# A graph network layer on one core: edge pairs taken earlier step by step, four node tiles finished among them, the last sum queued ahead of two linears

## The chip, the core and the metric

One core of a Trainium2 chip. The metric is the device time in microseconds; the kernel before took 907.19 us, the median of three runs (906.26 to 907.55).

## What is computed

Each of 106,250 edges has a source, a target (the edges are sorted by target) and one of three types. For each type, the message of an edge is the ReLU of a linear map of its source's row; a node's three sums of messages and the ReLU of its own row go through a linear map chosen by the node's type, and the result is added to twice the row (once in the layer, once around it) and normalised over its 128 features.

```python
src = node_feature[edge_src]
parts = [relu(node_feature)]
for t in range(3):
    msg = relu(src @ W_e[t].T + b_e[t])
    msg = where((edge_type == t)[:, None], msg, 0)
    parts.append(segment_sum(msg, edge_dst, num_segments=6250))
agg = concatenate(parts, axis=1)
for t in range(3):
    o = agg @ W_n[t].T + b_n[t]
    updated = where((node_type == t)[:, None], o, updated)
x = layernorm(x + (updated + node_feature))
```

## The kernel before

Nodes lie in 49 tiles of 128 rows (NT = 49, the last shorter). Setup (to about 100 us) writes a table in HBM with the message of each node for each type, while GpSimd gathers 71 chunks of 128 rows of x for the "early" edges, the last 9,050 in order.

The first 97,200 edges are 90 rows of 1,080. In each row the edges of a node to itself are handled apart (the "selfs"), 128 edges with a high source number are "dense" (their x rows are picked by one-hot matmuls from an SBUF copy of the last 1,280 nodes, so they are not gathered), and 896 edges at most are left, seven chunks of 128. Two rows make one of NI = 45 iterations: 14 gathers of 128 message rows each (L719), in four groups (quarters) of 3, 4, 3 and 4. A quarter is numbered q = 4j + g.

In quarter q TensorE sums the group with one-hot matrices (sum_group, L1605), and then does what the fixed schedule puts there. GpSimd may gather group (j, g) only after the sum of group (j-1, g), since the buffer is the same. VectorE makes the one-hot of the next iteration (L1217) and adds the sums into the accumulators at a base column that is read from a table into a register (add_to, L1229; load_bases).

Beside this run the pairs. One dense pair (256 dense edges) an iteration, and one early pair in each of the first NE = 36: a turn (dense_turn L1623, early_turn L1567), masks by type on VectorE a quarter later, the matmuls that make the messages three quarters after the turn (L1636 to L1640, L1579 to L1584), a ReLU on ScalarE, and a sum and its addition after them (ADD_LATER = 5). turn_at gives the quarter of pair r; pick_at that of its picking. LEAD_FROM and LEAD_STEP make the dense pairs from 36 on come every third quarter, so that the last is turned in quarter 171.

Node tiles are finished when no sum can reach them. Tiles 0 to 40 follow the iterations at fixed quarters (tile_step), with a turn of x (finish_turn), transposes of the selfs (place_selfs), the addition of accumulators and selfs into stage (finish_acc on VectorE, L1362), a linear of nine or more matmul instructions (linear_open L1679, L1680, linear_types L1687), the choice by node type and the statistics (finish_h, L1332 to L1340), the square root on ScalarE (finish_sd, L883) and the scaling (finish_y, L1346, L1348). Tiles 41, 42, 43 and 44 are left to last_iteration, whose order is written out by hand on each engine. Only early edges reach the four extra tiles, 45 to 48; they follow the early pairs, at quarters 151, 157, 163 and 169, in the order 48 to 45, through a set of buffers of their own (z = 1), which tile 44 uses after them. On ScalarE the roots in last_iteration are taken in the order of tiles 40, 41, 42, 43, 44; its end is:

```python
                finish_sd(Z0_TILES - 1)
                finish_sd(0, 3)
                finish_sd(KE, 1)
```

SyncE's queue is one list: loads of types and dense lists for the pairs, x rows and selfs for tiles, stores. At its end (L641 to L648) it stores tile 43, reads the control flag (which says if the input fits the plan) into a register, stores tile 44 and waits for all stores.

## Time and profile before

| | us |
|---|---|
| median of three runs | 907.19 (906.26 to 907.55) |
| the profiled execution | 908.36 |
| its span, first to last instruction | 906.6 |
| TensorE matmuls busy | 717.5 |
| GpSimd busy | 674.5 |
| VectorE busy | 614.0 |
| ScalarE busy | 145.8 |

Mean granted TensorE clock 0.909 of full speed. PE is TensorE's matmuls, PEld its weight loads, DVE VectorE, ACT ScalarE, POOL GpSimd, SPq the transfers that SyncE issues. A row of a timeline gives the start and the duration in us, the engine, the line of the program, the operation, what is written from what, how many instructions are merged, and in brackets the idle time before and what ended it. Instructions overlap in a pipeline, so that starts lie closer together than durations.

### The profile page before, as it was taken

To read this page: it belongs to the slowest core of one execution; us is meant where nothing else is said; L and a number is where in the kernel's file an instruction comes from. 1 tells how busy PE (TensorE), PEld (TensorE's weight loads), DVE (VectorE), ACT (ScalarE), POOL (GpSimd) and SP (SyncE) were. 2 spreads that over 40 slices of the span, in tenths; PEclk is the share of its full clock that TensorE was granted. 3 is DMA by queue.
4 is the path that set the end of the run, shared out by engine and by line. 5 is a ranking of instruction groups with operands and counts; after the bars stand their busy time and mean duration, and the time that the engine had idled before them with its cause. 6 is when DMAs were issued, how large, how long until landed. Compare 5 with 4: busy or idle time off the path is not lost.

```text
span 906.6 us, 13972 instructions
## 1 busy us (share of the span) xinstructions
PE 717.5 (79%) x4555; PEld 601.7 (66%) x4555; DVE 614.0 (68%) x1468; ACT 145.8 (16%) x397; POOL 674.5 (74%) x718
## 2 busy tenths in 40 slices
PE   5593066896998888888888889889887798889796
PEld 3362065785877776676677777778666677778674
DVE  6999988467676557556656666665765476757756
ACT  3293100111111101101111010111111011112120
POOL 7777777777777777777777777777777777777771
PEclk9796558799999989999999999989999898989999
DMA  8495532343543344333443344335335533434321
GB/s 251 145 313 154 138 96 77 97 111 51 146 118 105 97 109 106 96 110 90 99 122 92 94 105 113 94 94 123 95 96 128 146 69 103 110 77 121 81 53 50
DMA packets 71985, 101.39 MB, mean 112 GB/s; under 512 B 18057, under 2 KB 55437, under 8 KB 71915
## 3 DMA queue, kind: packets, MB, share of 16 engines
q0 software_dynamic: 22432, 45.99, 21.9%
q1 hardware_dynamic: 46781, 50.45, 18.7%
q10 hardware_dynamic: 2702, 4.08, 1.6%
q8 instruction: 37, 0.61, 0.3%
q14 instruction: 33, 0.27, 0.1%
HBM read 87.47 MB, written 12.97 MB: 111 GB/s over the span
## 4 chain that ended last, share of the span: by engine, by line
POOL 50%; PE 20%; issue 17%; DMA 6%; DVE 5%; SPq 0%; DVEq 0%; POOLq 0%
POOL tab L719 47%; DMA tab<-message_table,idx_t 5%; PE ps L1605 4%; PE ps L1687 3%; PE ps L1623 3%; POOL xg L715 3%; PE ps L1529 2%; PE ps L1680 1%; PE ps L1640 1%; DMA dst_raw<-in_dst 1%; PE ps L1636 1%; DVE h L1335 1%; PE ps L1648 1%; DVE first_wide L999 1%; PE ps L1530 1%
## 5 line engine op out<-in xcount | busy, mean ns | idle before, releaser
L719 POOL DMA_INDIRECT tab<-message_table,idx_t x630 | 595.9, 946 | 192.0 <-issue 186.8
L1605 PE MATMUL ps<-work,tab 128*128 128x126 f32 x1260 | 183.7, 289 | 111.5 <-DMA tab<-message_table,idx_t 87.3
L1217 DVE TENSOR_TENSOR work<-key_t,ps 128x378 f32<-128x378 f32 (+1 forms) x180 | 108.8, 606 | 228.9 <-PE ps L1605 226.8
L1605 PEld LDWEIGHTS ps<-work,tab 128*128 128x128 f32 x1260 | 165.3, 201 | 128.3 <-issue 84.2
L1229 DVE TENSOR_TENSOR acc<-ps,acc 128x126 f32 (+1 forms) x306 | 96.2, 314 | 30.6 <-DVE acc L1229 7.2
L1687 PE MATMUL ps<-wn_t,stage 128*128 128x384 f32 x282 | 98.6, 486 | 0.0
L715 POOL DMA_INDIRECT xg<-in_x,esrc_t x67 | 72.6, 1084 | 20.4 <-issue 17.1
L1687 PEld LDWEIGHTS ps<-wn_t,stage 128*128 128x128 f32 x282 | 53.6, 190 | 37.4
L1623 PE MATMUL ps<-first_wide,tab 128*128 128x128 f32 x450 | 65.3, 299 | 4.6 <-DVE first_wide L1293 4.6
L1623 PEld LDWEIGHTS ps<-first_wide,tab 128*128 128x128 f32 x450 | 61.5, 215 | 5.0 <-issue 5.0
L862 ACT ACTIVATE stage<-ps 128x128 f32<-128x128 f32 x47 | 13.1, 278 | 309.9 <-PE ps L1687 291.4
L1623 PE MATMUL ps<-dense_f,tab 128*128 128x128 f32 x450 | 60.7, 285 | 0.0
L1623 PEld LDWEIGHTS ps<-dense_f,tab 128*128 128x128 f32 x450 | 57.5, 203 | 0.0
L1335 DVE SCALAR_TENSOR_TENSOR h<-ps,mask,h 128x128 f32<-128x128 f32 x147 | 51.6, 351 | 5.2
L1579 PE MATMUL ps<-we_t,emsg 128*128 128x128 f32 x216 | 36.5, 313 | 23.3 <-issue 19.1
L1579 PEld LDWEIGHTS ps<-we_t,emsg 128*128 128x128 f32 x216 | 31.7, 220 | 25.9 <-issue 21.4
L883 ACT ACTIVATE sd<-mv,eps 128x1 f32<-128x1 f32 x49 | 14.4, 294 | 208.3 <-DVE mv L1340 208.3
L1636 PE MATMUL ps<-we_t,order_f 128*128 128x128 f32 x270 | 45.5, 314 | 3.0 <-DVE acc L1229 3.0
L1529 PE MATMUL ps<-we_t,work 128*128 128x384 f32 x98 | 42.9, 521 | 3.3 <-DVEq L961 3.2
L1640 PE MATMUL ps<-we_t,order_f 128*128 128x128 f32 x270 | 44.7, 304 | 0.0
L1636 PEld LDWEIGHTS ps<-we_t,order_f 128*128 128x128 f32 x270 | 41.4, 228 | 4.2 <-issue 3.6
L849 ACT ACTIVATE dense_f<-ps 128x256 f32<-128x256 f32 x45 | 17.3, 384 | 163.8 <-PE ps L1640 163.8
(255 smaller groups left out, 1046.7 us busy)
## 6 DMA issues: line engine op xcount, KB each, us to landing
tab<-message_table,idx_t POOLq DMA_INDIRECT x630, 3.5
message_table<-tab SPq DMA_DIRECT2D x24, 384.0 KB, 4.0
dst_raw<-dense_types SPq DMA_DIRECT2D x45, 192.0 KB
wn_raw<-message_table SPq DMA_DIRECT2D x22, 384.0 KB, 3.3
src_wide<-dense_lists SPq DMA_DIRECT2D x45, 128.0 KB, 3.3
we_raw<-early_types SPq DMA_DIRECT2D x18, 192.0 KB
be_b<-early_types SPq DMA_DIRECT2D x18, 192.0 KB
xg<-in_x SPq DMA_DIRECT2D x11, 256.0 KB, 4.0
```

The lines of the kernel that those rows point to most:

```text
L715: pool.indirect_dma_start(xg[:, q, :], None, x, bass.IndirectOffsetOnAxis(ap=rows, axis=0)).then_inc(x_gathered, 16)
L719: pool.indirect_dma_start(msg[:, slot, :], None, table, bass.IndirectOffsetOnAxis(ap=rows, axis=0)).then_inc(signal, 16)
L1217: dve.tensor_tensor(hot[:, first:first + n, :].rearrange("p c (t w) -> p c t w", w=WIN), keys.broadcast_to((P, n, T, WIN)), iota_win.rearr ...
L1229: dve.tensor_tensor(cols, sums.rearrange("p (t c) -> p t c", t=T), cols, ALU.add).then_inc(added, 1)
L1335: fin_link(dve.scalar_tensor_tensor(h[z][:, :], lin_bank(z, nth)[:, t * D:(t + 1) * D], mask[:, t, at(tile)], h[z][:, :], ALU.mult, ALU.ad ...
L1529: pe.matmul(ps[:, MSG_PS + i, 0:T * D], xt[:, par, i, :], we_t[:, :], start=True, stop=False)
L1579: pe.matmul(early_made[:, 0, :], exm[:, 0, t, :], we_t[:, t * D:(t + 1) * D], start=(t == 0), stop=False)
L1605: ins = pe.matmul(sums_bank(j, g), msg[:, column, :], hot[:, column, :], start=(c == 0), stop=(c == n - 1))
L1623: ins = pe.matmul(dxt_ps[:, :, s * DENSE:(s + 1) * DENSE], dx[:, (SETS - 1 - s) * DT + k, :], donehot[s][:, k, :, :], start=(k == 0), stop ...
L1636: pe.matmul(dmsg_ps[:, 0, :], dxm[:, 0, t, :], we_t[:, t * D:(t + 1) * D], start=(t == 0), stop=False)
L1640: ins = pe.matmul(dmsg_ps[:, 1, :], dxm[:, 1, t, :], we_t[:, t * D:(t + 1) * D], start=False, stop=(t == T - 1))
L1687: ins = pe.matmul(lin, stage[z][:, i, :], wn_t[:, i, :], start=False, stop=(i == T))
```

## The change

- Pairs: pair r, dense and early alike, is turned in quarter 4r + 3 less one quarter for each five pairs, up to eight. The early pairs' other steps are now given as distances from the turn (4 for the ReLU, 5 for the sum, 6 for the addition). Base registers are loaded for the next pair after each pair, and four for the iteration.
- Extra tiles: in the order 45 to 48, each after the early pair from which on nothing reaches it (13, 21, 30 and 35), at quarters 66, 93, 127 and 146; linears at 70, 98, 130 and 150. Self rows and x are turned together (turn_extra) into other columns of bank 2, the bank of the pairs' turns; the linear uses bank 7, that of the tiles. Both get waits for it. Loads and stores are one for each tile, in slots of xg that are free then.
- A limit for each early pair (elimit, an iota) replaces one limit for all in the check of the plan.
- The end: TensorE, VectorE and SyncE have another order in the last iteration. Numbers such as KE, 1 stand for tile 44; 0, 3 for 43; Z0_TILES - 1 for 42.

```diff
...
-ORDER = [NT - 1 - n for n in range(NZ)]
+ORDER = [NA + 1 + n for n in range(KE)] + [NA]
...
-LIN_PS, FIN_XT_PS = (7, 6, 2, 5), (5, 6, 5, 3)
-LAST_LIN_PS = 4
+LIN_PS, FIN_XT_PS = (7, 7, 2, 5), (5, 2, 5, 3)
+LAST_LIN_PS, LAST_FIN_XT_PS = 4, 6
+XT_AT = (0, T * P, 0, 0)
...
-LEAD_FROM, LEAD_STEP = NE, 3
+LEAD, LEAD_EVERY = 8, 5
 def turn_at(r):
-    return NG * min(r, LEAD_FROM) + NG - 1 + LEAD_STEP * max(r - LEAD_FROM, 0)
+    return NG * r + NG - 1 - min(LEAD, r // LEAD_EVERY)
...
+E_RELU_LATER, E_SUM_LATER, E_ADD_LATER = 4, 5, 6
...
-EXTRA_FROM, EXTRA_STEP = NG * (NE + 1) + 3, 6
-EXTRAS = {EXTRA_FROM + EXTRA_STEP * k: k for k in range(KE)}
...
+LIMIT_STEP = 15
+LIMIT_FIRST = MAIN // 17 - 30
+PAIR_OF = [min(NE - 1, max(0, -(-((NA + 2 + n) * P - LIMIT_FIRST) // LIMIT_STEP) - 1)) for n in range(KE)]
+FIRST_EXTRA = 16
+def extra_at(n):
+    ready = turn_at(PAIR_OF[n]) + E_ADD_LATER
+    r = next(r for r in range(NI) if turn_at(r) + 1 >= ready and turn_at(r) >= NG * FIRST_EXTRA)
+    return turn_at(r) + 2
+EXTRA_AT = [extra_at(n) for n in range(KE)]
+LINEAR_AT = [next(q for q in range(at + 2, at + 6) if q % NG == 2) for at in EXTRA_AT]
+EXTRAS = {at: n for n, at in enumerate(EXTRA_AT)}
+EXTRA_LINEAR = {at: n for n, at in enumerate(LINEAR_AT)}
+SLOT_OF = [EXTRA_AT[n] // NG + 8 if n < KE - 1 else NT for n in range(KE)] + [NT + 1 + T]
+LOAD_LAST = NI - 5
...
+            def load_extra(n):
+                tile, slot = ORDER[n], SLOT_OF[n]
+                rows = min(P, N - tile * P)
+                sp.wait_ge(e_turned, min(NE, (slot + T + 2) // 2))
+                sp.dma_start(xg[0:rows, slot, :], x[tile * P:tile * P + rows, :]).then_inc(fin_x[1], 16)
+                sp.dma_start(self_rows(tile),
+                             table[tile * P * T:(tile * P + rows) * T, :].rearrange("(p t) d -> p t d", t=T)
+                             ).then_inc(self_extra, 16)
+            def store_extra(n):
+                tile, slot = ORDER[n], SLOT_OF[n]
+                rows = min(P, N - tile * P)
+                sp.wait_ge(fin_y[1], n + 1)
+                sp.dma_start(out[tile * P:tile * P + rows, :], xg[0:rows, slot, :]).then_inc(stored[1], 16)
...
+                for n in range(KE):
+                    if j == EXTRA_AT[n] // NG - 2:
+                        load_extra(n)
+                    if j == (LINEAR_AT[n] + 3) // NG + 1:
+                        store_extra(n)
+                if j == LOAD_LAST:
+                    load_extra(KE)
...
+            sp.wait_ge(ctl_set, 1)
+            need = sp.value_load(ctl[0:1, 0:1], min_val=0, max_val=1)
+            store_extra(KE)
             sp.wait_ge(fin_y[3], 1)
             store_fin(NA - 1)
-            sp.wait_ge(ctl_set, 1)
-            need = sp.value_load(ctl[0:1, 0:1], min_val=0, max_val=1)
-            sp.wait_ge(fin_y[1], NZ)
-            store_fin(NA, 1, 1)
             sp.wait_ge(stored[0], 16 * STORES)
-            sp.wait_ge(stored[1], 16 * 3)
...
+            pool.iota(elimit[:, :], pattern=[[0, 1]], base=LIMIT_FIRST, channel_multiplier=LIMIT_STEP,
...
-                dve.tensor_scalar(estats[:, 2:3], estats[:, 0:1], -1.0, float(EARLY_BACK), ALU.mult, ALU.add)
+                dve.wait_ge(limits_set, 1)
+                dve.tensor_tensor(estats[:, 2:3], elimit[:, :], estats[:, 0:1], ALU.subtract)
...
                 r = dense_step(q, ADD_LATER)
                 if r is not None:
-                    dense_add(r, bases_of[NG:NG + SIDES] if r <= LEAD_FROM else load_bases(r + 2, NG, NG + SIDES))
+                    dense_add(r, pair_base[0:SIDES])
+                    if r >= NE:
+                        pair_base = load_bases(r + 1, NG, NG + SIDES)
                 if dense_step(q, MASK_LATER) is not None:
                     dense_mask(dense_step(q, MASK_LATER))
-                if g == 0 and 1 <= j <= NE:
-                    early_mask(j - 1)
+                if early_step(q, MASK_LATER) is not None:
+                    early_mask(early_step(q, MASK_LATER))
...
+                i = early_step(q, E_ADD_LATER)
+                if i is not None:
+                    early_add(i, pair_base[SIDES])
+                    pair_base = load_bases(i + 1, NG, NG + SIDES + (i + 1 < NE))
...
+            def last_iteration(j, bases_of, pair_base):
                 dve.wait_ge(group_summed, NG * j + 1)
-                dense_add(j, load_bases(j + 2, NG, NG + SIDES))
+                dense_add(j, pair_base)
                 for g in range(NG):
...
                 dve.wait_ge(group_summed, NG * j + 4)
                 add_sums(j, 3, bases_of[3])
+                finish_acc(ORDER[KE], KE, 1, ALL_ADDS)
                 finish_acc(NA - 1, 0, 3, ALL_ADDS)
-                finish_acc(ORDER[KE], KE, 1, ALL_ADDS)
                 finish_h(SPLIT + 1, Z0_TILES - 1)
+                finish_h(ORDER[KE], KE, 1, slot=SLOT_OF[KE])
+                finish_y(SPLIT + 1, Z0_TILES - 1)
                 finish_h(NA - 1, 0, 3)
-                finish_y(SPLIT + 1, Z0_TILES - 1)
-                finish_h(ORDER[KE], KE, 1)
+                finish_y(ORDER[KE], KE, 1, slot=SLOT_OF[KE])
                 finish_y(NA - 1, 0, 3)
-                finish_y(ORDER[KE], KE, 1)
...
+                extras = sum(at < turn_at(i) for at in EXTRA_AT)
+                if extras:
+                    pe.wait_ge(stage_acc[1], extras)
...
+            def turn_extra(n):
+                tile, bank = ORDER[n], fin_bank(1, n)
+                rows = min(P, N - tile * P)
+                pe.wait_ge(fin_x[1], 16 * (n + 1))
+                pe.wait_ge(self_masked[1], n + 1)
+                pe.wait_ge(d_masked, sum(turn_at(r) < EXTRA_AT[n] for r in range(NI)))
+                pe.wait_ge(e_masked, sum(turn_at(i) < EXTRA_AT[n] for i in range(NE)))
+                part = self_rows(tile)
+                for t in range(T):
+                    ins = pe.transpose(ps[:, bank, t * P:t * P + rows], part[:, t, :], ident[0:rows, 0:rows])
+                ins.then_inc(self_placed[1], 1)
+                pe.transpose(ps[:, bank, XT_AT[1]:XT_AT[1] + P], xg[:, SLOT_OF[n], :], ident[:, :]
+                             ).then_inc(fin_xt[1], 1)
...
+                if behind is not None:
+                    pe.wait_ge(fin_var[1 - z], behind)
...
                 if q in EXTRAS:
-                    k = EXTRAS[q]
-                    if k == 0:
-                        pe.wait_ge(added, ADDED["early", NE - 1, 0])
-                    else:
-                        pe.wait_ge(fin_var[1], k)
-                    finish_turn(ORDER[k], k, 2, 1, first=k == 0)
+                    turn_extra(EXTRAS[q])
                 t = tile_step(q, 1)
                 if t is not None:
                     place_selfs(t, t)
-                if q - 1 in EXTRAS:
-                    place_selfs(ORDER[EXTRAS[q - 1]], EXTRAS[q - 1], 1)
                 t = tile_step(q, LINEAR_LATER)
                 if t is not None:
-                    finish_linear(t, first=t == 0)
-                if q - LINEAR_LATER in EXTRAS:
-                    finish_linear(EXTRAS[q - LINEAR_LATER], 1, first=EXTRAS[q - LINEAR_LATER] == 0)
-                if g == 0 and 2 <= j <= NE + 1:
-                    early_sum(j - 2)
+                    extras = sum(at < q for at in LINEAR_AT)
+                    finish_linear(t, first=t == 0, behind=extras if extras else None)
+                if q in EXTRA_LINEAR:
+                    n = EXTRA_LINEAR[q]
+                    done = sum(tile_step(before, LINEAR_LATER) is not None for before in range(q))
+                    finish_linear(n, 1, first=n == 0, behind=done)
+                if early_step(q, E_SUM_LATER) is not None:
+                    early_sum(early_step(q, E_SUM_LATER))
...
                 pe.wait_ge(hot_ready, NG * NI)
                 pe.wait_ge(d_hot, NI)
+                pe.wait_ge(added, ADDED["main", j, 1])
                 linear_open(KE, 1)
+                sum_group(j, 3)
                 finish_linear(Z0_TILES - 1)
-                linear_open(0, 3, first=True)
-                pe.wait_ge(added, ADDED["main", j, 1])
-                sum_group(j, 3)
-                linear_types(0, 3)
                 linear_types(KE, 1)
+                finish_linear(0, 3, first=True)
...
```

## Rows read from the trace of the kernel before

**Rows 1.** The page, part 1, TensorE: share of the span:
```profile
PE 717.5 (79%) x4555; PEld 601.7 (66%) x4555; DVE 614.0 (68%) x1468; ACT 145.8 (16%) x397; POOL 674.5 (74%) x718
```

**Rows 2.** The waits, GpSimd before its gathers: us in total, times, longest:
```profile
POOL tab L719 <- issue: 186.8, 613, 0.3
POOL tab L719 <- PE ps L1605: 5.2, 17, 0.3
```

**Rows 3.** The gathers of messages by line: ns min/median/max, first and last start:
```profile
L719 POOL DMA_INDIRECT tab<-message_table,idx_t x630: 940/945/1064, 101.4 to 888.1; - x158
```

**Rows 4.** Timeline of TensorE at the end: start us, us, engine, line:
```profile
893.97 1.05 PE L1605 MATMUL ps<-work,tab 128*128 128x126 f32 x8
...
896.08 2.20 PE L1687 MATMUL ps<-wn_t,work 128*128 128x384 f32 x6 [1.06 <-DVE work L1362]
```

**Rows 5.** Timeline of VectorE and ScalarE at the end:
```profile
895.15 0.29 DVE L1229 TENSOR_TENSOR acc<-ps,acc 128x126 f32 x1 [1.81 <-PE ps L1605]
...
901.09 1.12 DVE L1335 SCALAR_TENSOR_TENSOR h<-ps,mask,h 128x128 f32<-128x128 f32 x3
...
902.86 0.29 ACT L883 ACTIVATE sd<-mv,eps 128x1 f32<-128x1 f32 x1 [2.11 <-DVE mv L1340]
...
902.91 0.35 DVE L1348 TENSOR_SCALAR xg<-h,mv,rstd 128x128 f32<-128x128 f32 x1
...
903.39 0.35 DVE L1348 TENSOR_SCALAR xg<-h,mv,rstd 128x128 f32<-128x128 f32 x1
```

**Rows 6.** Timeline of SyncE's queue, the last two stores:
```profile
903.28 0.33 SPq L523 DMA_DIRECT2D out<-xg  x1
...
904.54 0.34 SPq L523 DMA_DIRECT2D out<-xg  x1
```

**Rows 7.** Timelines of TensorE and GpSimd, first group and the gather it frees:
```profile
115.88 1.65 PE L1605 MATMUL ps<-work,tab 128*128 128x126 f32 x6 [23.18 <-DVE work L1217]
...
118.92 0.95 POOL L719 DMA_INDIRECT tab<-message_table,idx_t  x1 [0.30 <-issue]
```

**Rows 8.** The chain that ended last, 890 to 896 us: start, duration, what:
```profile
891.39 1.94 PE ps L1687 x6
...
893.32 0.16 PE ps L1679
...
893.48 0.65 PE ps L1680 x2
...
894.13 0.90 PE ps L1605 x8
```

**Rows 9.** Timeline of GpSimd at the start:
```profile
2.02 0.13 POOL L694 IOTA limit<- 90x2 f32 x1
...
3.25 1.10 POOL L715 DMA_INDIRECT xg<-in_x,esrc_first  x1 [0.40 <-DMA esrc_first<-in_src]
```

**Rows 10.** Chain at 432 and 835 us, timelines of GpSimd and TensorE at 270:
```profile
835.50 3.47 DMA tab<-message_table,idx_t
...
839.11 1.13 PE ps L1605 x8
...
432.68 4.08 DMA tab<-message_table,idx_t
...
270.16 0.94 POOL L719 DMA_INDIRECT tab<-message_table,idx_t  x1 [0.30 <-issue]
...
272.90 0.91 PE L1605 MATMUL ps<-work,tab 128*128 128x126 f32 x6 [1.43 <-DMA tab<-message_table,idx_t]
```

**Rows 11.** Windows: busy PE, PEld, DVE, ACT, POOL; PEclk; DMA; GB/s. Linear matmuls by line:
```profile
853.00:856.00 3.00, 0.53 (x5) 0.29 (x4) 2.80 (x7) 0.00 (x0) 2.39 (x3) 1.00 0.79 244
...
858.00:859.00 1.00, 0.21 (x1) 0.24 (x2) 0.70 (x3) 0.21 (x1) 0.93 (x1) 0.76 0.25 66
...
865.00:866.00 1.00, 1.00 (x9) 1.00 (x9) 0.00 (x0) 0.00 (x0) 0.69 (x2) 0.82 0.13 33
...
L1687 PE MATMUL ps<-wn_t,stage x282: 485/486/486, 185.7 to 899.7; 128*128 128x384 f32 x141
```

More of the change, by code:

```diff
@@ L161, in dense_step, with early_step @@
     return TURNS.get(q - later)
-EXTRA_FROM, EXTRA_STEP = NG * (NE + 1) + 3, 6
-EXTRAS = {EXTRA_FROM + EXTRA_STEP * k: k for k in range(KE)}
+def early_step(q, later):
+    i = TURNS.get(q - later)
+    return i if i is not None and i < NE else None
 ACC_LATER, LINEAR_LATER, H_LATER, SD_LATER, Y_LATER = 2, 4, 5, 6, 7
-assert max(EXTRAS) + Y_LATER <= NG * (NI - 1)
+LIMIT_STEP = 15
[12 more added lines that the diff above has]
+LOAD_LAST = NI - 5
+assert all(EXTRA_AT[n + 1] > LINEAR_AT[n] + 3 for n in range(KE - 1)) and LINEAR_AT[-1] + 3 < NG * (NI - 1)
+assert all(LIMIT_FIRST + LIMIT_STEP * (PAIR_OF[n] + 1) >= (NA + 2 + n) * P for n in range(KE - 1))
+assert PAIR_OF[-1] == NE - 1 and SLOT_OF[KE] + 1 + T <= ET
 def tile_step(q, later):
@@ L454, in self_rows, with fin_bank @@
                 return rows_of[:, tile // 2 % 2, tile % 2, :].rearrange("p (t d) -> p t d", d=D)
-            first = NT + T * (NT - 1 - tile)
+            first = SLOT_OF[ORDER.index(tile)] + 1
             return xg[0:min(P, N - tile * P), first:first + T, :]
+        def fin_bank(z, nth):
+            return LAST_FIN_XT_PS if z == 1 and isinstance(nth, int) and nth == KE else FIN_XT_PS[z]
         def load_x(engine, b, par):
@@ L532, in load_selfs @@
                              ).then_inc(self_got[m % 2], 16)
-            def load_extra_selfs():
-                for tile in ORDER:
-                    rows = min(P, N - tile * P)
-                    sp.dma_start(self_rows(tile),
-                                 table[tile * P * T:(tile * P + rows) * T, :].rearrange("(p t) d -> p t d", t=T)
-                                 ).then_inc(self_extra, 16)
             def iteration(j):
-                if 2 <= j < NE:
-                    sp.wait_ge(e_made, j - 1)
-                    load_early_types(j)
+                for i in range(2, NE):
+                    if j == (turn_at(i - 2) + MAKE_LATER) // NG + 1:
+                        sp.wait_ge(e_made, i - 1)
+                        load_early_types(i)
                 for r in range(2, NI):
@@ L554, in iteration @@
                     if j == tile + 1:
+                        before = sum(SLOT_OF[n] < tile + tiles for n in range(KE))
+                        if before:
+                            sp.wait_ge(stored[1], 16 * before)
                         sp.wait_ge(e_turned, (tile + tiles + 1) // 2)
@@ L871, in mask_selfs @@
                 else:
-                    act.wait_ge(self_extra, 16 * NZ)
+                    act.wait_ge(self_extra, 16 * (ORDER.index(tile) + 1))
                 if tile == 0:
@@ L902, in quarter @@
                     mask_selfs(ORDER[EXTRAS[q + 2]])
-                if g == 3 and 1 <= j <= NE:
-                    early_relu(j - 1)
+                if early_step(q, E_RELU_LATER) is not None:
+                    early_relu(early_step(q, E_RELU_LATER))
             def last_iteration():
@@ L1357, in finish_acc @@
                 dve.wait_ge(self_placed[z], nth + 1)
+                if z == 1 and nth < KE:
+                    dve.wait_ge(stage_xt[z], nth + 1)
                 sums = acc[:, :, tile * P:(tile + 1) * P]
@@ L1619, in dense_turn @@
                     pe.wait_ge(e_masked, min(j, NE))
+                extras = sum(at < turn_at(j) for at in EXTRA_AT)
+                if extras:
+                    pe.wait_ge(stage_acc[1], extras)
                 for s in range(SETS):
@@ L1669, in finish_turn, with linear_open @@
                     pe.wait_ge(stage_acc[z], nth)
-                pe.transpose(ps[:, FIN_XT_PS[z], 0:P], xg[:, at(tile), :].rearrange("p a d -> p (a d)"), ident[:, :]
+                slot = tile if z != 1 else SLOT_OF[nth]
+                pe.transpose(ps[:, fin_bank(z, nth), XT_AT[z]:XT_AT[z] + P], xg[:, at(slot), :].rearrange("p a d -> p (a d)"), ident[:, :]
                              ).then_inc(fin_xt[z], 1)
-            def linear_open(nth, z=0, first=False):
+            def linear_open(nth, z=0, first=False, behind=None):
                 lin = lin_bank(z, nth)
@@ L1688, in linear_types, with finish_linear @@
                 ins.then_inc(fin_lin[z], 1)
-            def finish_linear(nth, z=0, first=False):
+            def finish_linear(nth, z=0, first=False, behind=None):
                 if z == 1:
                     pe.wait_ge(stage_acc[z], nth + 1)
-                linear_open(nth, z, first)
+                linear_open(nth, z, first, behind)
                 linear_types(nth, z)
```

86 lines of the change are left out of this document (38 added, 48 removed).

## The prediction

> **What bounds the kernel now.** I read the page first: TensorE has the largest busy share, 79% [rows 1], and that does not say what bounds. The waits of GpSimd do: before its 630 gathers of message rows it was idle 0.3 us each, nearly all of it its own issue; a TensorE sum ended such a gap 17 times, never a longer one than 0.3 us [rows 2]. The gathers as a group close the question: the first began at 101.4, the last at 888.1 [rows 3], so 786.7 / 629 = 1.25 us per gather, and one gather of 0.945 with its gap of 0.3 is 1.25. So from 101 to 889 us the run is one uninterrupted row of gathers with no wait of another engine in it. What the change takes off TensorE or VectorE there is worth nothing by itself; it can cost, if a gather has to wait, or help the last 18.5 us (888.1 to the span's end, 906.6).
>
> In those the reader should see three things. The sum of the last group started at 893.97, behind all the linear work queued ahead of it on TensorE [rows 4]. VectorE had been free since 893.34, waited 1.81 us for that sum, and worked without a gap from 895.15 to 903.74 [rows 5]. SyncE issued the store of tile 43 at 903.28, right behind its rows, and that of tile 44, ready at 903.74, only at 904.54 [rows 6]: between the two stands the read of the control flag into a register.
>
> **The change, part by part.**
>
> *Pairs run ahead.* Before, pair r is turned in quarter 4r+3, and from pair 36 every third quarter; after, pair r comes min(8, r//5) quarters earlier, and the last is in quarter 171 in both. No matmul is added. From quarter 147 on, 7 pairs are turned instead of 9. Cost 0, covered by the gathers as long as GpSimd isn't held. How thin that cover can be: the first group's sum ended at 115.88 + 1.65 = 117.53, and the gather that needs it began at 118.92 [rows 7], 1.4 us of room. There pairs 0 to 4 keep their places, and only one load of three registers is added ahead of the loop. In the middle some quarters now hold the making of a pair and a tile's linear, 2.75 us more [rows 8]; the end becomes thinner.
>
> *Four extra tiles early.* Their turns move from quarters 151, 157, 163, 169 to 66, 93, 127, 146, each with 2.75 us of linear [rows 8] and its transposes. The new waits: TensorE waits for the tile's loads, its masked rows and the masks of earlier pairs; the next pair's turn waits for VectorE's addition of the extra tile; the linears of both kinds wait for each other's statistics, since they share a bank. Queued behind each are the sums, and behind these the gathers. The next turn lies two quarters behind an extra tile in all four places, and the loads are queued on SyncE two iterations ahead, 28 gathers or 35 us [rows 3]. I take 0; a held gather is rival D. On SyncE the two stores of these tiles leave the last microseconds, where they were issued while the last gather was in flight; what that gives lies within the bounds of the landing below.
>
> *Base registers.* VectorE loads a pair's bases after the pair before, instead of with the iteration: as many values, beside the gathers, and not behind the last sum in either kernel. 0.
>
> *One more iota on GpSimd* ahead of its first gather, and a limit read by VectorE: 0.13 us by its like, against 0.40 us for which that gather waited for its indices [rows 9]. 0, at most 0.1.
>
> *The last sum moved ahead.* This is the term. After, the order is: open tile 44, last sum, linear 42, types of 44, all of linear 43. First S, the end of that sum, which now waits for the last gather alone. No row shows that landing, so I bound it by sums that waited for theirs. A gather begun at 835.50 took 3.47, and its sum began at 839.11, 3.61 after the gather; another took 4.08, with the same 0.14 behind it 4.22; a group of three chunks began 272.90 - 270.16 = 2.74 after its last gather [rows 10]. I take 3.61, since it is of the same group of four chunks and late in the run. With two matmuls for the last chunk (a quarter of 0.90, 0.23 [rows 8]) S = 888.1 + 3.61 + 0.23 = 891.9, with bounds of 891.1 and 892.6. TensorE is there in time: ahead of the old sum stood a linear (2.75) and an opening (0.81) that are now behind it, and 893.97 - 3.56 = 890.4. The old sum ended at 893.97 + 1.05 = 895.0 [rows 4], so it gains 3.1 us.
>
> Not all of this arrives. After S TensorE has 2.75 + 1.94 + 2.75 = 7.44 us in a row [rows 8]. Before, two types of about 2 us were left [rows 4], and VectorE was the bound. Linear 43 is done at S + 7.44 = 899.4, and 0.12 later (the sum ended at 895.03, the add began at 895.15) VectorE has it: 899.5. VectorE's own work up to there is what it was, 901.09 - 895.15 = 5.94 us [rows 5], less than the 7.44, so TensorE sets the end now. From the last tile's first multiply-add to the square root on ScalarE it is 902.86 - 901.09 = 1.77 us [rows 5]: 901.3.
>
> *A term that goes the other way.* VectorE now finishes 44 ahead of 43, but ScalarE's order is not changed: it still takes the root of 43 first, which depends on the very last statistics, and the root of 44 behind it. So the finishing of 44, which could have lain beside the root of 43, waits too. A root is 0.29 and I put the second 0.2 behind it (an estimate between 0.16 and 0.29); then 0.59 from root to the first tile's end (903.15 to 903.74) and 0.48 to the second's (903.26 to 903.74) [rows 5]: 901.3 + 0.29 + 0.2 + 0.59 + 0.48 = 902.8, where it would be 902.2 with the roots swapped. Against 903.74 a gain of 0.9 is left of the 3.1.
>
> *The flag read moved.* It now stands ahead of both last stores. The store that ends last is issued 0.02 us behind its tile, as that of 43 was, instead of 904.54 - 903.74 = 0.80: a gain of 0.78. The read's own time, below 0.93 (903.28 + 0.33 to 904.54 [rows 6]), is covered: tile 42 is ready some 3 us before the others. From the last issue to the span's end it stays 906.6 - 904.54 = 2.06.
>
> **Sum.** 902.8 + 0.02 + 2.06 = 904.9 against the span's 906.6: -1.7, by the bounds of S -2.5 and -1.0. The profiled execution took 908.36, 1.8 of it outside the span, and lies 1.2 above the median of 907.19; I carry the difference over: 907.19 - 1.7 = 905.5.
>
> **Rivals.**
>
> *A: the last rows land as fast as those of the three-chunk groups* (S = 891.1, -2.5, 904.7). For: row 272.90 [rows 10], and two stores are gone from that moment. Against: the same group elsewhere took 3.6 and more.
>
> *B: little more than the flag read is saved* (906.4 to 907.2). Then S is 893 or later: a late landing, or TensorE held just before it. For: VectorE finished its earlier tiles at 893.34 only [rows 5]; where a matmul needs an add queued behind these, the chain shifts. Against: the tile's sums that the first linear needs came before these.
>
> *C, slower: the clock.* TensorE was busy for 0.53 of 3 us from 853 on, then its granted clock fell from 2.4 to 1.2 GHz during 858 and rose again only during 865, though it was busy throughout by then [rows 11]. With less work left for the last iterations it will idle more there, and the 7.44 us are now the bound. If it falls at S, 7 us do the work of 3.5: 905.5 + 3.5 = 909.0; with all 7.44 at half clock, 912.9. It decides once TensorE runs slow for over 2 x 1.7 = 3.4 us after S. Against: the linear matmuls were never slow in 282, 485 to 486 ns each [rows 11], and the idling before S, 890.4 to 891.7, is short.
> The Trainium skill (TensorE: Matmul & The Clock Gate, Part 1) says that the clock is gated by how busy the array has been lately, and that the lower rate is the state it falls back to. The trace agrees in kind, and by this rule a thinner end can only lose: C.
>
> *D: a gather is held* by a new wait. A hold of 5 us costs it less the room: 3.6 with the 1.4 us of the first group [rows 7], nothing where the room is larger; with half of it 907.3. For: several new waits at four places. Against: loads 35 us ahead.
>
> *E: the first parts don't do anything for the time* is the forecast itself.
>
> **Chances.** A measurement can tell 0.2% from no change, 1.8 us, and the forecast lies just inside. Forecast 0.55, of which 0.22 gains over 1.8; A 0.22; B 0.11; C 0.06; D 0.06. Faster by over 0.2%: 0.22 + 0.22 = 0.44. Slower: C, half of D, and 0.04 for costs that no row shows, 0.13. Within: 0.43. The range takes the forecast, A with 1 us for its own scatter, B and the near half of D: 903.7 to 907.6.
>
> **What would show it.** Gathers from 101.4 to 888.1 without a wait; the last sum split in two, ending between 891.1 and 892.6; behind it linear 42, the types of 44 and linear 43 without a gap, at 2.4 GHz; the roots of 43 and 44 side by side after the last statistics; both last stores within 0.5 us. I am wrong if the last gather begins later than 888.6 (D), if the granted clock is 1.2 GHz after S (C), or if S is later than 892.6 (B).

## The result, and the profile after

| | before | after |
|---|---|---|
| median, us | 907.13 (4 runs) | 980.47 (4 runs, 977.34 to 983.19) |
| ratio, 95% interval | | 1.0809 [1.0774, 1.0843] |
| profiled execution, us | 908.36 | 977.34 |
| its span, us | 906.6 | 975.5 |
| TensorE clock granted, mean | 0.909 | 0.868 |

The change makes the kernel 8% slower, where 905.5 us was forecast and no more than 907.6 expected. The page, part 1, of the changed kernel, against [rows 1]:

```profile
PE 747.0 (77%) x4555; PEld 622.6 (64%) x4555; DVE 617.8 (63%) x1468; ACT 143.8 (15%) x397; POOL 673.8 (69%) x719
```

As many instructions on TensorE and VectorE; TensorE's take 29.5 us more, which is clock. The waits of GpSimd, of TensorE and of VectorE (us in total, times, longest), and the gathers as a group, against [rows 2, 3]:

```profile
POOL tab L753 <- issue: 182.9, 600, 0.3
POOL tab L753 <- PE ps L1652: 81.2, 30, 5.8
...
PE ps L1626 <- issue: 50.4, 22, 7.1
...
PE ps L1652 <- DVE acc L1264: 25.2, 8, 3.9
...
PE ps L1747 <- DVE mv L1375: 22.5, 6, 6.1
...
DVE work L1252 <- PE ps L1652: 272.2, 86, 10.0
```

```profile
L753 POOL DMA_INDIRECT tab<-message_table,idx_t x630: 938/944/1041, 101.6 to 959.3; - x158
```

The gathers no longer stand in one row. Thirty of them waited for a sum (L1652, which was L1605), 81.2 us in all, which is 72.2 us beyond the issue gap of 0.3 each. The last begins at 959.3 where it began at 888.1: 71.2 later. From there to the span's end it is 975.5 - 959.3 = 16.2 where it was 18.5: 2.3 shorter. 71.2 - 2.3 is the whole of the span's 68.9. So the new end does what it should, and the gathers lose thirty times that. TensorE stood 50.4 us in front of L1626, the making of an early pair's messages (19.1 before), and VectorE waited 272.2 us for sums (226.8 before).

Iteration by iteration, no gather is held up to iteration 13; from 14 to 21 the holds are 1.5, 2.9, 6.5, 6.0, 11.0, 2.3, 5.8 and 9.3 us; from 22 to 25 none; then 4.6 in 26 and 22.2 in 33 to 39; none behind it. The lead moves a pair's turn through the iteration: a lead of 0, 4 or 8 puts it in quarter 3 of one, 1 or 5 in quarter 2, 2 or 6 in quarter 1, 3 or 7 in quarter 0. Turns lie in quarter 1 or 0 in iterations 10 to 19 and 29 to 38, and the holds follow them, late because the room is used up first and because a gather waits for a sum of the iteration before. Only the hold in 26 comes with turns in quarter 2. It belongs to the second extra tile: its linear waited for a tile's statistics, and the next tile's linear for those of the extra tile:

```profile
584.63 0.32 PE L1747 MATMUL ps<-bn_parts,pick_parts 128*128 128x384 bf16 x1 [3.17 <-DVE mv L1375]
602.09 0.43 PE L1747 MATMUL ps<-bn_parts,pick_parts 128*128 128x384 bf16 x1 [4.52 <-DVE mv L1375]
```

What happens there is seen in one iteration with the turn in quarter 0. TensorE, and beneath it VectorE, of the changed kernel:

```profile
477.10 1.62 PE L1626 MATMUL ps<-we_t,emsg 128*128 128x128 f32 x6 [7.13 <-issue]
...
483.17 0.83 PE L1652 MATMUL ps<-work,tab 128*128 128x126 f32 x6
...
484.76 2.10 PE L1755 MATMUL ps<-wn_t,stage 128*128 128x384 f32 x6
...
486.91 1.28 PE L1673 MATMUL ps<-first_wide,tab 128*128 128x128 f32 x10
488.03 1.28 PE L1673 MATMUL ps<-dense_f,tab 128*128 128x128 f32 x10
489.14 0.90 PE L1698 MATMUL ps<-first_wide,dense_f 128*128 128x216 f32 x4
489.88 1.05 PE L1652 MATMUL ps<-work,tab 128*128 128x126 f32 x8
...
499.92 1.62 PE L1626 MATMUL ps<-we_t,emsg 128*128 128x128 f32 x6 [6.66 <-issue]
...
504.98 1.65 PE L1690 MATMUL ps<-we_t,order_f 128*128 128x128 f32 x6
```

```profile
490.97 0.68 DVE L1252 TENSOR_TENSOR work<-key_t,ps 128x504 f32<-128x504 f32 x1 [6.05 <-PE ps L1652]
491.56 0.82 DVE L1328 TENSOR_TENSOR first_wide<-src_wide,ps 128x640 f32<-128x640 f32 x1
...
494.69 0.95 DVE L1307 TENSOR_TENSOR emsg<-ps,be_b 128x768 f32<-128x768 f32 x1
...
496.54 1.12 DVE L1370 SCALAR_TENSOR_TENSOR h<-ps,mask,h 128x128 f32<-128x128 f32 x3
...
499.53 0.29 DVE L1264 TENSOR_TENSOR acc<-ps,acc 128x126 f32 x1 [0.20 <-DVE acc L1264]
```

In quarter 0 TensorE does a tile's linear, the pair's turn (20 matmuls) and the dense sum before it comes to the sum of quarter 1 (489.88). VectorE waits 6.05 us for that sum. Then it does picks, masks, additions and a tile's statistics in a row, 8.9 us, with the early pair's addition (499.53) last. TensorE is to make the next pair's messages (499.92), which by the program must come after that addition, and waits 6.66 us for it. Each engine stands while the other works. That is a ring, and its round can be added up: the distance from the making before (477.10) to this one (499.92) is 22.8 us. The making of both kinds, mostly at 1.2 GHz, takes 6.1 of it (477.10 to 483.17), TensorE's work from there until VectorE has the sum of quarter 1 takes 7.8 (483.17 to 490.97), and VectorE takes 8.9 (490.97 to 499.82, with 0.1 to hand over). An iteration of 14 gathers takes 17.5.

With the turn in quarter 1 it is another link: the sum of quarter 0 waits up to 3.9 us for the last addition of an iteration before, which on VectorE stands behind picks and both masks. The round is 20.3 us (340.72 to 360.99).

### The profile page after: what moved, and what is told of

It is laid out like the page before. It is cut to its first block, busy times and chain, and to the rows that moved or that the text cites. A ratio compares the mean times of both kernels' runs of the same rounds, so it can differ in the third digit from the quotient of the medians.

```text
span 975.5 us, 14051 instructions
## 1 busy us (share of the span) xinstructions
PE 747.0 (77%) x4555; PEld 622.6 (64%) x4555; DVE 617.8 (63%) x1468; ACT 143.8 (15%) x397; POOL 673.8 (69%) x719
## 3 DMA queue, kind: packets, MB, share of 16 engines
q1 hardware_dynamic: 46861, 50.45, 17.6%
## 4 chain that ended last, share of the span: by engine, by line
PE 51%; DVE 23%; issue 12%; POOL 10%; DMA 1%; DVEq 1%; SPq 0%; POOLq 0%; ACT 0%; ACTq 0%
POOL tab L753 10%; PE ps L1652 10%; PE ps L1755 9%; PE ps L1673 8%; PE ps L1631 4%; PE ps L1626 3%; PE ps L1690 3%; PE ps L1748 3%; PE ps L1686 3%; PE ps L1698 2%; DVE first_wide L1328 2%; DVE emsg L1307 2%; DVE dense_f L1328 2%; DVE acc L1264 2%; DVE src_wide L1098 1%
## 5 line engine op out<-in xcount | busy, mean ns | idle before, releaser
L1252 DVE TENSOR_TENSOR work<-key_t,ps 128x378 f32<-128x378 f32 (+1 forms) x180 | 109.4, 609 | 285.5 <-PE ps L1652 272.2
L1652 PE MATMUL ps<-work,tab 128*128 128x126 f32 x1260 | 185.5, 292 | 68.8 <-DVE acc L1264 25.2
L1652 PEld LDWEIGHTS ps<-work,tab 128*128 128x128 f32 x1260 | 172.3, 207 | 79.2 <-DVE acc L1264 26.8
L1755 PE MATMUL ps<-wn_t,stage 128*128 128x384 f32 x282 | 112.5, 541 | 0.0
L1755 PEld LDWEIGHTS ps<-wn_t,stage 128*128 128x128 f32 x282 | 62.3, 221 | 48.6 <-issue 20.2
L1626 PE MATMUL ps<-we_t,emsg 128*128 128x128 f32 x216 | 38.2, 322 | 53.8 <-issue 50.4
L1626 PEld LDWEIGHTS ps<-we_t,emsg 128*128 128x128 f32 x216 | 33.4, 226 | 61.7 <-issue 55.5
L1673 PE MATMUL ps<-first_wide,tab 128*128 128x128 f32 x450 | 62.1, 289 | 5.6 <-DVE first_wide L1328 5.6
L1673 PEld LDWEIGHTS ps<-first_wide,tab 128*128 128x128 f32 x450 | 58.3, 204 | 7.0 <-issue 5.9
L1686 PE MATMUL ps<-we_t,order_f 128*128 128x128 f32 x270 | 46.7, 320 | 5.0 <-DVE order_f L1338 4.2
L1690 PE MATMUL ps<-we_t,order_f 128*128 128x128 f32 x270 | 48.0, 320 | 0.0
L1748 PE MATMUL ps<-wn_t,stage 128*128 128x384 f32 x94 | 47.6, 595 | 0.0
```

The lines of the kernel that those rows point to most:

```text
L1252: dve.tensor_tensor(hot[:, first:first + n, :].rearrange("p c (t w) -> p c t w", w=WIN), keys.broadcast_to((P, n, T, WIN)), iota_win.rearr ...
L1626: pe.matmul(early_made[:, 0, :], exm[:, 0, t, :], we_t[:, t * D:(t + 1) * D], start=(t == 0), stop=False)
L1652: ins = pe.matmul(sums_bank(j, g), msg[:, column, :], hot[:, column, :], start=(c == 0), stop=(c == n - 1))
L1673: ins = pe.matmul(dxt_ps[:, :, s * DENSE:(s + 1) * DENSE], dx[:, (SETS - 1 - s) * DT + k, :], donehot[s][:, k, :, :], start=(k == 0), stop ...
L1686: pe.matmul(dmsg_ps[:, 0, :], dxm[:, 0, t, :], we_t[:, t * D:(t + 1) * D], start=(t == 0), stop=False)
L1690: ins = pe.matmul(dmsg_ps[:, 1, :], dxm[:, 1, t, :], we_t[:, t * D:(t + 1) * D], start=False, stop=(t == T - 1))
```

## The experiments

Each was run beside the kernel before on the same chip, with a median for that of 907.2 in the first batch (tail_only to quick_leads), 907.34 in the second (lead_1 to mask_same), 906.26 in the third (lead3_add_earlier to late_extras) and 907.13 in the fourth.

**tail_only**: the kernel before, with only the new orders of the last iteration (TensorE, VectorE, the flag read on SyncE). **tail_roots**: the same, with the root of tile 44 ahead of that of 43.

```diff
+                pe.wait_ge(added, ADDED["main", j, 1])
                 linear_open(KE, 1)
+                sum_group(j, 3)
                 finish_linear(Z0_TILES - 1)
-                linear_open(0, 3, first=True)
-                pe.wait_ge(added, ADDED["main", j, 1])
-                sum_group(j, 3)
-                linear_types(0, 3)
                 linear_types(KE, 1)
+                finish_linear(0, 3, first=True)
...
-                finish_sd(0, 3)
                 finish_sd(KE, 1)
+                finish_sd(0, 3)
```

> The kernel before with the new orders of the last iteration alone (TensorE's last sum ahead of two linears, VectorE's 44 ahead of 43, SyncE's flag read ahead of both stores); leads, extra tiles, loads as before. My prediction's sum: -1.7 us, so 905.5, with the last sum's end at 891.9 (891.1 to 892.6). Rival B: only the flag read, 906.4. If the end itself had been at fault in the change: above 907.

> The same, and ScalarE takes the root of tile 44 ahead of that of 43. If the root term of the prediction is right, 0.5 to 0.8 us less than the run before it, about 904.8. If the roots don't matter: the same as the run before it.

Measured: tail_only 905.8 (11 runs), ratio 0.9990 [0.9981, 0.9999]; tail_roots 905.44 (11 runs), 0.9982 [0.9973, 0.9991]. Of tail_only, with a last gather at 887.7, TensorE's last sum and last linear, the two roots and the last tile's rows:

```profile
889.69 1.45 PE L1605 MATMUL ps<-work,tab 128*128 128x126 f32 x8 [0.33 <-DMA tab<-message_table,idx_t]
...
896.45 2.10 PE L1687 MATMUL ps<-wn_t,work 128*128 128x384 f32 x6
...
900.43 0.48 ACT L883 ACTIVATE sd<-mv,eps 128x1 f32<-128x1 f32 x2 [4.38 <-DVE mv L1340]
...
901.60 0.35 DVE L1348 TENSOR_SCALAR xg<-h,mv,rstd 128x128 f32<-128x128 f32 x1
```

And of tail_roots the roots of 44 and 43, and the last rows:

```profile
897.64 0.29 ACT L883 ACTIVATE sd<-mv,eps 128x1 f32<-128x1 f32 x1 [1.66 <-DVE mv L1340]
900.37 0.29 ACT L883 ACTIVATE sd<-mv,eps 128x1 f32<-128x1 f32 x1 [2.43 <-DVE mv L1340]
...
900.89 0.35 DVE L1348 TENSOR_SCALAR xg<-h,mv,rstd 128x128 f32<-128x128 f32 x1
```

The sum ends at 889.69 + 1.45 = 891.14, the last linear at 898.55, 7.41 behind it; the last rows are done at 901.95, 10.81 behind it. With the roots swapped it is 901.24 against a sum that ended at 891.07, 10.17 behind: 0.64 less in these two traces. The medians differ by 0.36 only, less than the 0.5 to 0.8 expected, and their intervals overlap.

**old_leads**: the changed kernel with the turns of before. **quick_leads**: no lead to pair 16, then one quarter more for each pair to a lead of 4 at pair 20, 4 to pair 37, and 8 from pair 41.

```diff
-    return NG * r + NG - 1 - min(LEAD, r // LEAD_EVERY)
+    return NG * min(r, NE) + NG - 1 + 3 * max(r - NE, 0)
...
+    return NG * r + NG - 1 - (max(0, min(4, r - 16)) + max(0, min(4, r - 37)))
```

> The changed kernel with the old quarters of the pairs (4r+3, from pair 36 every third) and all else new: extra tiles in iterations 17, 24, 33 and 38, their waits, loads and limits, base registers, last iteration. Theory L, the leads put the work of a pair into the same quarters as that of a tile, and TensorE and VectorE wait for each other in a ring: the loss of 73 us goes nearly whole, 905 to 912. Theory X, the waits of the extra tiles: it stays, 960 and more. Theory C, the granted clock alone: as long as the work per iteration is the same, most of it stays.

> The changed kernel with a lead that passes the three bad places fast: 0 up to pair 16, then 1, 2, 3, 4 at pairs 17 to 20, 4 up to 37, and 5 to 8 at 38 to 41. Turns lie in quarter 3 of an iteration but for two short passes. Theory L with the place in the iteration as the cause: below 920. If it is the lead's size that hurts (pairs that come early), about half of the loss stays, 930 to 950. Theory X: 960 and more.

Measured: old_leads 906.5 (8 runs), ratio 0.9994 [0.9983, 1.0004]; quick_leads 919.9 (2 runs), 1.0146 [1.0127, 1.0164]. The waits of GpSimd in old_leads, then in quick_leads:

```profile
POOL tab L753 <- PE ps L1652: 9.4, 21, 2.2
```

```profile
POOL tab L753 <- PE ps L1652: 20.1, 15, 5.3
```

One line put back takes all of the loss away, with the extra tiles early as in the changed kernel (their quarters are counted from the turns, so they come 3 to 6 quarters later than there). In quick_leads the gathers are held 15.6 us, nearly all in iterations 20 and 21, right behind the pairs whose turns pass quarters 1 and 0 (18 and 19). From iteration 22 to 37, all with a lead of 4, none is held: a turn a whole iteration early costs nothing.

**lead_1, lead_2, lead_3**: one constant lead for pairs 5 to 36 (lead_2 and lead_3 get there in as many pairs), after them up to 8 as in the changed kernel. One run each.

```diff
-    return NG * r + NG - 1 - min(LEAD, r // LEAD_EVERY)
+    return NG * r + NG - 1 - (max(0, min(1, r - 4)) + max(0, min(7, r - 36)))
...
+    return NG * r + NG - 1 - (max(0, min(2, r - 4)) + max(0, min(6, r - 36)))
...
+    return NG * r + NG - 1 - (max(0, min(3, r - 4)) + max(0, min(5, r - 36)))
```

> The changed kernel with a lead of one quarter for all pairs from 5 to 36, and one more for each pair after that. Turn in quarter 2, masks in 3, messages made in 1 of an iteration. Theory L: this place is harmless, as in iterations 5 to 13 of the changed kernel: 903 to 912. If the number of pairs that run ahead counts and not the place, some of the loss is here too.

> The same with two quarters: turn in quarter 1, masks in 2, messages made in 0, beside the tile's linear. In the changed kernel TensorE took 20.3 us for such an iteration (340.7, 361.0, 381.4). Theory L: 32 such pairs, 2.8 us over the 17.5 of the gathers each, less 8 to 10 us of room: 970 to 1000. A theory of the passes (only where the lead steps does a wait fall badly): below 925.

> The same with three: turn in quarter 0 beside the tile's linear, masks in 1 beside finish_h, messages made in 3. In the changed kernel such an iteration took 22.8 us (477.1 to 499.9). Theory L: 32 x 5.3 less 10, 1050 to 1080, the worst of the three. The theory of the passes: below 925.

Measured: 905.75, 1005.31 and 1081.49. GpSimd's waits for sums are 5.4, 113.9 and 197.5 us. Beyond the issue gaps gathers are held 0.9, 100.7 and 174.7 us in total, in lead_2 3.0 in nearly every iteration from 8 to 36 and in lead_3 about 5.3. The two times above 1000 are 5.3 and 1.5 us above their ranges. TensorE's waits in two iterations running of lead_2, with the start of its making between them, and one wait of lead_3:

```profile
503.31 1.65 PE L1652 MATMUL ps<-work,tab 128*128 128x126 f32 x6 [3.92 <-DVE acc L1264]
...
509.86 0.83 PE L1626 MATMUL ps<-we_t,emsg 128*128 128x128 f32 x6
...
523.85 1.65 PE L1652 MATMUL ps<-work,tab 128*128 128x126 f32 x6 [3.92 <-DVE acc L1264]
```

```profile
519.24 1.62 PE L1626 MATMUL ps<-we_t,emsg 128*128 128x128 f32 x6 [7.14 <-issue]
```

The two places of the changed kernel stand here alone and steady: quarter 1 has a round of 523.85 - 503.31 = 20.5 us, 3.0 over the gathers; quarter 0 costs 5.3; quarter 2 nothing.

Nearly all of the 3.0 of quarter 1 looks like clock. From the sum of quarter 0 through the tile's linear to the making, TensorE takes 509.86 - 503.31 = 6.55 us, at a granted clock of 0.54 of full speed. In the kernel before the same stretch, at full clock, lies between these two rows:

```profile
492.76 0.90 PE L1605 MATMUL ps<-work,tab 128*128 128x126 f32 x6
...
496.35 0.60 PE L1593 MATMUL ps<-ehot,early_selected 128*128 128x126 f32 x4
```

That is 3.6 us. Without the 3.0 between them the round would be 17.6 us, as long as the gathers. This is an estimate from the rows; no run of this place at full clock was made.

**mask_same**: the changed kernel with the dense masks in the quarter of the turn instead of one later.

```diff
-MASK_LATER, MAKE_LATER, SUM_LATER, ADD_LATER = 1, 3, 4, 5
+MASK_LATER, MAKE_LATER, SUM_LATER, ADD_LATER = 0, 3, 4, 5
```

> The changed kernel with the masks of a pair in the quarter of its turn instead of the next, so that VectorE need not wait for the sum of the next quarter before it masks. If the loss is the ring in which VectorE idles 6 us for a sum queued behind TensorE's turn and linear, and TensorE then idles 6.7 us for VectorE: well over half goes, below 940. If TensorE's work in one quarter is too much by itself: it stays within 15 us of 980.

Measured: 991.81 (2 runs), ratio 1.0926 [1.0879, 1.0974], gathers held 88.5 us and now from iteration 11 on. The forecast of the ring (below 940) missed. MASK_LATER rules the early masks too, and what VectorE has to do in a round stays the same; the wait only moved, to the early pair's one-hot: TensorE's wait for it was 17.4 us in 4 waits and is

```profile
PE ps L1640 <- DVE ehot L1294: 58.3, 26, 5.0
```

**lead3_add_earlier**: lead_3, with the early pair's addition one quarter earlier. It also lets the later extra tiles start a pair earlier, since their place is counted from that addition.

```diff
-E_RELU_LATER, E_SUM_LATER, E_ADD_LATER = 4, 5, 6
+E_RELU_LATER, E_SUM_LATER, E_ADD_LATER = 4, 5, 5
```

> The run with three quarters of lead (1081.5 us), and VectorE adds an early pair's sum one quarter earlier, ahead of finish_h. In each iteration TensorE idled 6.7 us ahead of the next pair's matmuls, until that addition (VectorE, one add, 499.53, TensorE from 499.92). Ring theory, this addition is the link from VectorE back to TensorE: some 4 us less an iteration (finish_h 2.0, a one-hot 0.5, two adds 0.7, an own add), 26 iterations, 970 to 1000. If the link is another (masks, types' loads): no change.

**lead3_fill**: lead_3, with matmuls that nothing reads issued on TensorE while it would wait to make messages, once in each of 26 iterations, to keep it busy.

```diff
                 if early_step(q, MAKE_LATER) is not None:
-                    early_make(early_step(q, MAKE_LATER))
+                    i = early_step(q, MAKE_LATER)
+                    if 8 <= i <= 33:
+                        pe.wait_ge(added, ADDED["dense", i - 1, SIDES - 1])
+                        for _ in range(20):
+                            pe.matmul(ps[:, DENSE_PS, SIDES * T * DW:512], ident[:, :], we_t[:, 0:512 - SIDES * T * DW],
+                                      start=True, stop=True)
+                    early_make(i)
```

> The same run, and TensorE, where it idles 6.7 us, now does 20 matmuls (128 by 80, in two passes) whose results nobody reads, ahead of the early pair's matmuls of pairs 8 to 33. They fill some 3 to 5 us. Ring theory: TensorE idles there, so the filler costs nothing. If the clock has a part (TensorE ran at 1.2 GHz behind each idle stretch, the pair's matmuls took 6.9 us instead of 3.5): up to 3 us less an iteration, 1000 to 1050. Theory of TensorE's capacity (too much work in an iteration): slower, by up to 26 x 4 us.

**lead3_thin**: lead_3, with two of the three node types left out of the linears of tiles 0 to 40 and the tiles that share their buffers; the output lacks these types.

```diff
-                for i in range(1, T + 1):
+                for i in range(T if z == 0 else 1, T + 1):
```

> The same run, but two of the three types' matmuls of a tile's linear (set 0) are left out, 4 of 9 instructions, 1.3 us, so the output lacks these parts. The linear stands ahead of the sum for which VectorE waits, so by the ring theory each iteration gets 1.3 us shorter: 1081 - 27 x 1.3 = 1046 (1035 to 1055). If VectorE and TensorE were merely loaded too much in total, TensorE being 80% busy: less than 10 us.

Measured, against lead_3's 1081.49: 1003.9, 1058.31 and 1032.73 (one run each), which is 77.6, 23.2 and 48.8 less. All three lie outside their ranges, by 3.9 and 8.3 above and 2.3 below. TensorE's wait for the making, in lead_3, lead3_add_earlier and lead3_fill:

```profile
PE ps L1626 <- issue: 170.6, 31, 7.1
```

```profile
PE ps L1626 <- issue: 82.5, 23, 3.9
```

```profile
PE ps L1626 <- issue: 50.7, 27, 7.1
```

The addition is a link: freed of it the wait is about half as long, and almost half of the loss over the kernel before (174 us) goes. The linear, done by TensorE alone while VectorE waits, is another: 1.3 us of matmuls at 2.4 GHz less in each round brings 1.8 (48.8 in 27 rounds). And the clock is a part. A window of 890 us of lead_3, then of lead3_fill (busy PE, PEld, DVE, ACT, POOL; clock; DMA share; GB/s):

```profile
110.00:1000.00 890.00, 645.60 (x3970) 559.59 (x3970) 472.83 (x1151) 88.41 (x288) 540.77 (x573) 0.82 0.32 82
```

```profile
110.00:1000.00 890.00, 745.67 (x5156) 659.09 (x5157) 488.64 (x1193) 91.86 (x300) 556.75 (x591) 0.92 0.33 85
```

123 us of added matmuls made the kernel 23 us faster, since those that matter ran less often at half clock: the making at 528.74 in lead3_fill took 0.91 where it took 1.62 in lead_3. The 23 us are a balance. In steady rounds of lead3_fill the making comes every 20.3 us and at full clock, where it came about every 22.8 us in lead_3:

```profile
549.07 0.91 PE L1626 MATMUL ps<-we_t,emsg 128*128 128x128 f32 x6 [1.27 <-issue]
569.40 0.91 PE L1626 MATMUL ps<-we_t,emsg 128*128 128x128 f32 x6 [1.27 <-issue]
```

So in such a round the clock is 2.5 us of the 5.3, and the other 2.8 are the ring itself, still longer than the gathers. Other rounds gained less, and near the extra tiles lead3_fill lost more than lead_3 (gathers held 10.8 and 6.8 us in iterations 18 and 19 against 8.9 and 2.3), and why is open.

**late_extras**: the changed kernel, with the first two extra tiles at quarters 97 and 108, where the lead is 4 or 5, instead of 66 and 93, out of the iterations in dispute.

```diff
-EXTRA_AT = [extra_at(n) for n in range(KE)]
+EXTRA_AT = [97, 108, 127, 146]
```

> The changed kernel, with the first two extra tiles at quarters 97 and 108 instead of 66 and 93, where pairs are in quarter 3 again (108: lead of 5). Theory X: the waits of the first two cost most of the 73 us: below 930. By theory L they cost what TensorE waits at their linears and turns, 6.1, 3.4 us and a share of the 4.7 in iteration 26, and only where the ring has eaten the room: 965 to 980.

Measured: 990.66 (2 runs), ratio 1.0931 [1.0899, 1.0963], gathers held 86.5 us. So the extra tiles are not what holds the gathers in iterations 14 to 21, though the linear of the first of them waits long for the statistics of a tile (450.17, 6.07 us, on L1747). Without them the holds there still are 44.9 us (45.3 with them). That the time came out above its range, and 10 us above the change, lies mostly behind: from iteration 27 to 32 gathers are held 15.6 us, with the turns in quarters 2 and 1, where the changed kernel has none there and 4.6 in 26. Just before and in that stretch TensorE waited twice before a tile's linear for the statistics of an extra tile, 5.60 us at 621.51 and

```profile
664.13 0.48 PE L1747 MATMUL ps<-bn_parts,pick_parts 128*128 128x384 bf16 x1 [5.61 <-DVE mv L1375]
```

So an extra tile is free or costs some microseconds, depending on where it lies.

**add_earlier**: the changed kernel with the addition one quarter earlier. As in lead3_add_earlier this moves the later extra tiles too, by four quarters. **lead_1_roots**: lead_1 with the roots swapped as in tail_roots.

> The changed kernel with one constant less: the early pair's addition comes five quarters after its turn instead of six. Theory of the ring (TensorE's making of a pair waits for the early addition, VectorE's sums wait behind TensorE's linear and turn): in the run with all pairs three quarters ahead this edit removed 77.6 of 174 us; the same share of the changed kernel's 73.3 us over the kernel before is 33, so 947, and 935 to 960 if the places two quarters ahead take a different share. If the early addition only mattered in that extreme schedule: 978 to 982, with the gathers held 72 us as in the changed kernel. If it were the whole of the loss: 906 to 908.

> The changed kernel with the dense and early pairs 5 to 36 one quarter ahead only (the pairs behind 36 catch up as in the changed kernel), and the root of tile 44 taken ahead of that of tile 43. Theory (only the place of the pair's turn costs time; the new last iteration is worth 1.4 to 1.7 us and the swap of the roots about 0.4): extras early, all the rest of the change, no gather held for more than about 1 us in total, 905.0 to 905.6, faster than the kernel before by 0.15 to 0.25 per cent. Rival: what the extras and the new waits add is paid in full somewhere else: 906.5 or more, no difference from the kernel before.

Measured: add_earlier 956.99 (2 runs), ratio 1.0552 [1.0531, 1.0573]; lead_1_roots 905.84 (11 runs), 0.9989 [0.998, 0.9998]. In add_earlier the gathers are held 51.3 us instead of 72.2. TensorE waits for the making and for the additions of sums:

```profile
PE ps L1652 <- DVE acc L1264: 28.8, 9, 3.9
...
PE ps L1626 <- issue: 10.8, 4, 3.6
```

The first link shrinks from 50.4 to 10.8, so it is a link in the changed kernel too. Of the 21 us of holds that go, 13.8 lie in iterations 14 to 21; 4.6 are the hold of iteration 26, which goes with the moved second extra tile. The second link (25.2 in the changed kernel, 28.8 now), that of quarter 1, is as it was, and it is part of what is left. Quarter 0 still costs too: there the making waits up to 3.6 us. A remedy of that second link alone was not tried. lead_1_roots came out 0.24 above its range: the turns a quarter early and the extras early bring nothing over tail_roots (905.44), whose interval overlaps. The lowest median of all is that of the kernel before with a new last iteration and the roots swapped.

## Why the prediction was wrong

**The step that failed** is *Pairs run ahead*: "Cost 0, covered by the gathers as long as GpSimd isn't held." It named the condition and did not work it out. The room was read at one place, 1.4 us at the first group, and the added work per quarter was taken by itself ("the making of a pair and a tile's linear, 2.75 us more"), as if TensorE's busy time decided. What decides is how long TensorE and VectorE take in turn, when each waits for the other's last result: rounds of 20.3 and 22.8 us against 17.5 us of gathers. Rival D had the right mechanism, a held gather, with a chance of 0.06 and a price of 3.6 at most; it sought the hold at four places of new waits, where it happens in fifteen iterations, in all but one of them by the moved turns. The size was wrong by a factor of twenty (72.2 us of holds against 3.6) because a hold was priced once: 5 us less the room. A ring longer than the gathers pays its excess in every round, and the room only once (pairs turn in quarter 1 from iteration 10 on, and the first gather is held in 14).

Could it have been seen before? For quarter 0, yes. The round above can be added up from rows of before. The making of both kinds took 3.5 us there at 2.4 GHz, from 501.10 to about 504.6:

```profile
501.10 0.83 PE L1579 MATMUL ps<-we_t,emsg 128*128 128x128 f32 x6
...
503.83 0.94 PE L1640 MATMUL ps<-we_t,order_f 128*128 128x128 f32 x6
```

The 7.8 and 8.9 are instructions that before has too, one by one, at the same length. That is 20.2, more than 17.5, with no guess on the clock, and lead3_fill's 20.3 bears it out; the clock adds 2.6 to it. For quarter 1 the estimate above gives some 17.6, about even with the gathers, and by it the rest of the 20.3 is the clock after each wait. Rival C had that mechanism and looked for it only behind the last sum.

*Extra tiles*: with the old turns 0 was right as far as can be measured, old_leads 906.5 against tail_only's 905.8. With the moved turns it was not quite: the wait that the text had named ("the linears of both kinds wait for each other's statistics") held the gathers 4.6 us in iteration 26, and cost more in late_extras. The first extra tile's linear also waited, 6.07 us, in a ring that was already late. *Base registers*, *iota*: the first gather begins at 101.6, within the bound.

*The last sum moved ahead*: right in each term to 0.5 us, read from tail_only. S forecast at 3.84 behind the last gather, measured 891.14 - 887.7 = 3.4. To linear 43's end 7.44, measured 7.41, the types' matmuls at their rate of before (2.10 for six), so rival C is out for the end of the run. From there to the last rows 3.5 was forecast, 3.4 measured. *The roots*: 0.6 forecast, 0.64 in the traces and 0.36 in the medians. The flag read ahead of both stores does what it should: in the changed kernel the last two are issued 0.45 apart, at 972.77 and 973.22, the latter as its rows end:

```profile
972.77 0.34 SPq L568 DMA_DIRECT2D out<-xg  x1
973.22 0.36 SPq L552 DMA_DIRECT2D out<-xg  x1
```

In sum -1.7 was forecast for all this and -1.4 measured in tail_only.

## What to carry to other kernels

When a change moves work between slots of a fixed schedule, follow one round in which two in-order engines wait for each other and add up the parts of both; busy shares don't show it, and an engine free for a third of the time can still be late. Compare that round with the period of what bounds the kernel: an excess is paid every time, so multiply it by the rounds. And try the places one at a time at a constant offset: two of four quarters cost nothing here, the other two 3.0 and 5.3 us a round. Leave room in such a sum for the clock: when TensorE waits in every round, part of its work in the round may run at half speed.

## What the runs showed of the hardware

A ring makes TensorE slow on top of late. After 6.66 us of idling its granted clock was 1.2 GHz for most of the work that followed, and the making there is on the ring: the window of the changed kernel, with the clock after the busy times, and a making at another place at 2.4 GHz (0.91 for the six that took 1.62 in the ring):

```profile
499.00:508.00 9.00, 8.08 (x42) 7.26 (x43) 2.66 (x7) 0.87 (x3) 4.40 (x5) 0.58 0.32 71
```

```profile
566.35 0.91 PE L1626 MATMUL ps<-we_t,emsg 128*128 128x128 f32 x6
```

A shorter wait did it too: in lead_2, behind a wait of 3.92 us in each round, the granted clock was 0.54 for the next 6.5 us. Filling the idle time with matmuls that nothing reads was a gain: a mean clock of 0.902 instead of 0.825, and 23 us.
